# First expert stage of a vision tower on Trainium2: looked-up units copied on chip, first two pairs interleaved

## The reference

```python
h = tok(x)                                     # shifted patches, layernorm, projection
h = h + attn(layernorm(h))                     # 12 heads, fake-quantised
h = h + ffn1(layernorm(h))                     # 8 experts, hidden 512, one expert per token
h = h + block(layernorm(h))                    # state-space block and its own MLP
h = h + ffn2(layernorm(h))                     # 8 experts, hidden 768, two experts per token
```

```python
route = softmax(hidden @ router_w + router_b); e = argmax(route)
out[token] = (silu(x @ w1[e]) * (x @ w2[e])) @ w3[e] * max(route)
```

## Time and profile before

| | us |
|---|---|
| runs | 360.35, 359.46, 364.96 |
| median of the three | 360.35 |
| the profiled execution, its own time | 361.43 |
| its span, first to last instruction | 359.7 |
| TensorE busy | 328.1 |
| VectorE busy | 184.2 |
| ScalarE busy | 136.9 |
| GpSimd busy | 90.5 |

### The profile page before, as it was taken

How to read it: one execution, slowest core, us unless ns; L and a number is a source line. 1 busy time by engine, 2 the same in 40 slices (tenths; PEclk the granted TensorE clock), 3 DMA queues, 4 the chain that set the end, 5 groups by cost and what they waited for, 6 DMA issues and landing times.

```text
span 359.7 us, 6821 instructions
## 1 busy us (share of the span) xinstructions
PE 328.1 (91%) x2564; PEld 252.3 (70%) x2564; DVE 184.2 (51%) x513; ACT 136.9 (38%) x282; POOL 90.5 (25%) x120
## 2 busy tenths in 40 slices
PE   4999998949987999999897988988999999999996
PEld 2999874527553445455674756757999999999995
DVE  3785797775561343467989533574123321521125
ACT  3999222871421122237981433331121121221220
POOL 8299814000014322102032020004223233222110
PEclk9999999977997899999999999999999999999999
DMA  7944349967959999170059993022299999999322
GB/s 235 397 87 104 70 138 273 267 153 220 235 144 254 270 289 243 33 178 20 0 118 294 250 238 90 18 58 58 58 287 284 266 266 274 251 255 248 99 74 86
DMA packets 32450, 64.56 MB, mean 179 GB/s; under 512 B 11009, under 2 KB 17698, under 8 KB 32418
## 3 DMA queue, kind: packets, MB, share of 16 engines
q1 hardware_dynamic: 30210, 59.38, 62.7%
q0 software_dynamic: 1920, 4.56, 4.8%
q10 hardware_dynamic: 288, 0.20, 0.2%
HBM read 59.46 MB, written 4.65 MB: 178 GB/s over the span
## 4 chain that ended last, share of the span: by engine, by line
PE 69%; DVE 12%; ACT 7%; POOL 6%; issue 3%; DMA 1%; another core or an unknown queue 0%; SPq 0%; DVEq 0%; ACTq 0%
PE ps L1850 12%; PE ps L1875 9%; PE ps L1862 7%; PE ps L1941 4%; PE ps L1658 4%; PE ps L1593 4%; PE ps L1974 3%; PE ps L1738 3%; PE ps L1664 2%; PE ps L1949 2%; PE ps L1827 2%; POOL tot L105 1%; PE ps L2152 1%; PE ps L1963 1%; POOL xsq L592 1%
## 5 line engine op out<-in xcount | busy, mean ns | idle before, releaser
L665 POOL DMA_INDIRECT xg<-token_x,src_id x22 | 21.4, 974 | 125.5 <-DVE src_id L1328 79.5
L1357 DVE TENSOR_TENSOR ht<-sg,ps 128x384 f32<-128x384 f32 (+1 forms) x48 | 23.8, 509 | 50.2 <-ACT sg L877 45.6
L1850 PE MATMUL ps<-xgt,wup 128*128 128x128 f32 x384 | 45.6, 275 | 1.5 <-ACT xgt L868 1.5
L1850 PEld LDWEIGHTS ps<-xgt,wup 128*128 128x128 f32 x384 | 44.8, 192 | 2.0 <-issue 2.0
L1593 PE MATMUL ps<-busy 128*128 128x512 bf16 x149 | 41.1, 390 | 4.5 <-POOL ident L575 4.5
L877 ACT ACTIVATE sg<-ps 128x384 f32<-128x384 f32 (+1 forms) x48 | 21.1, 455 | 50.3 <-PE ps L1862 32.7
L1601 PE MATMUL ps<-weff,xp 128*128 128x193 f32 x240 | 39.9, 327 | 0.1
L1601 PEld LDWEIGHTS ps<-weff,xp 128*128 128x128 f32 x240 | 39.2, 190 | 0.7 <-DVE weff L1012 0.7
L1875 PE MATMUL ps<-wdn,ht 128*128 128x192 f32 x192 | 35.2, 334 | 0.0
L672 POOL DMA_INDIRECT token_y<-ysb,row_id x20 | 19.7, 987 | 54.8 <-ACT ysb L884 54.5
L1875 PEld LDWEIGHTS ps<-wdn,ht 128*128 128x128 f32 x192 | 30.8, 190 | 1.8
(11 more groups left out here) (348 smaller groups left out, 563.8 us busy)
## 6 DMA issues: line engine op xcount, KB each, us to landing
wup<-in_m_w SPq DMA_DIRECT2D x16, 576.0 KB
wup<-in_m_w SPq DMA_DIRECT2D x48, 192.0 KB
wdn<-in_m_w SPq DMA_DIRECT2D x16, 576.0 KB
wup<-in_m_w SPq DMA_DIRECT2D x13, 384.0 KB, 6.2
wup<-in_m_w SPq DMA_DIRECT2D x39, 128.0 KB, 6.8
wdn<-in_m_w SPq DMA_DIRECT2D x13, 384.0 KB, 8.6
xw<-in_xw SPq DMA_DIRECT2D x2, 784.0 KB, 10.4
wall<-in_w_sh SPq DMA_DIRECT2D x2, 768.0 KB, 7.3
```

The costliest lines, as they stand in the source:

```text
L665: g.indirect_dma_start(xg[:, j, :], None, token_x[m], bass.IndirectOffsetOnAxis(ap=src_id[:, j:j + 1], axis=0))\
L1357: v.tensor_tensor(ht[:, j % 2, s, 0:half], sg[:, s, 0:half], ups, ALU.mult)\
L1850: mm(ps[:, 2 * s + g, c * P:c * P + P], up[:, col:col + P], xgt[:, 0, j * P:j * P + P], start=(c == 0), stop=False)
```

## The change

Three things change in the first expert stage.

1. Units 8 to 11 no longer come from memory. Once the weights of all own units have arrived, SP copies them from the buffer of the own unit with the looked-up expert to buffers 8 to 11, with two DMAs a unit from SBUF to SBUF. To address that buffer by a register, the nine buffers of the arena become one tensor `w1`; the layout in memory stays.
2. Before SP loads unit 12 (from memory, as before), it waits until units 8 to 11 have arrived, since buffers 0 to 3 may be a copy's source. Semaphore values follow: two DMAs in place of five.
3. Pairs 0 and 1 are interleaved like all others. TensorE does pair 0's up products, three fill matmuls, the transposes of the first gathered group, two fill matmuls, and then pair 1's up products, and pair 0's across and down work inside that iteration. The wait for the remainder rows (`a_f1`) moves to `up_pair_rest(0)`. ACT and DVE follow the same order.

```diff
-W_LOADS = 5
+W_LOADS, C_LOADS = 5, 2
+WARM_ROWS = (3, 2)
...
+        w1 = sb("w1", [P, M1_LOW, UP + DOWN], scope=arena)
...
             b, uses = weight_uses(m, j)
-            return S[ARRIVED[b]], 16 * W_LOADS * uses + (16 if b >= 10 else 0)
+            if m == 0 and b >= E:
+                return S[ARRIVED[b]], 16 * C_LOADS + (16 if b >= 10 else 0)
+            return S[ARRIVED[b]], 16 * W_LOADS * uses
...
+            def copied_weights(j, e):
+
+                b, _ = weight_uses(0, j)
+                up, down = wbuf[0][b]
+                own = w1[:, bass.ds(e, 1), :].rearrange("p e n -> p (e n)")
+                sp.dma_start(up, own[:, 0:UP]).then_inc(S[ARRIVED[b]], 16)
+                sp.dma_start(down, own[:, UP:UP + DOWN].rearrange("p (c d) -> p c d", d=D)).then_inc(S[ARRIVED[b]], 16)
...
                     if j < E:
                         expert_weights(m, j)
+                        continue
+                    if m == 0 and j == E:
+                        for i in range(E):
+                            sp.wait_ge(*weights_here(0, i))
+                    if m == 0 and j == M1_BUFS:
+                        for i in range(E, M1_BUFS):
+                            sp.wait_ge(*weights_here(0, i))
+                    e = sp.value_load(te[0:1, j - E:j - E + 1], min_val=0, max_val=E - 1)
+                    if m == 0 and j < M1_BUFS:
+                        copied_weights(j, e)
                     else:
-                        expert_weights(m, j, sp.value_load(te[0:1, j - E:j - E + 1], min_val=0, max_val=E - 1))
+                        expert_weights(m, j, e)
```

ScalarE, VectorE and TensorE:

```diff
-                    if (m, j) == (0, 0):
-                        result(0)
-                    elif j >= (2 if m == 0 else 1):
+                    if j >= 1:
                         result(j - 1)
...
-                    if m == 0 and j >= 2:
+                    if m == 0 and j >= 1:
                         hidden_across(j - 1)
                     if j == 0:
                         product(0, 0)
-                        if m == 0:
-                            product(0, 1)
-                            hidden_across(0)
                         gathered(1)
-                        if m == 1:
-                            product(0, 1)
+                        product(0, 1)
...
                     pe.wait_ge(S["a_gt"], r["group_of"][j] + 1)
-                    if j == 0:
-                        pe.wait_ge(S["a_f1"], 2)
-                    else:
+                    if j > 0:
                         pe.wait_ge(S["v_gt"], r["group_of"][j])
...
                 def up_pair_rest(j):
 
+                    if j == 0:
+                        pe.wait_ge(S["a_f1"], 2)
...
                         if j == 0:
                             up_pair_rest(0)
-                            hidden_across(0)
-                            down_pair(0)
+                            keep_busy(2, WARM_ROWS[0])
                             gathered(1)
+                            keep_busy(2, WARM_ROWS[1])
                             continue
-                        if j >= 2:
-                            hidden_across(j - 1)
+                        hidden_across(j - 1)
...
                         up_pair_rest(j)
-                        if j >= 2:
-                            down_pair(j - 1)
+                        down_pair(j - 1)
```

More of the change, by code:

```diff
@@ L219, in build @@
         gate = sb("gate", [P, 2, TT])
[L222 to L230, removed]
+        arena = ExitStack()
+        w1 = sb("w1", [P, M1_LOW, UP + DOWN], scope=arena)
+        arena.close()
+        arena = ExitStack()
+        wbuf = [[(w1[:, b, 0:UP], w1[:, b, UP:UP + DOWN].rearrange("p (c d) -> p c d", d=D)) for b in range(M1_LOW)],
+                [(sb(f"wup{b}", [P, 3 * M2_H], scope=arena), sb(f"wdn{b}", [P, M2_H // P, D], scope=arena))
+                 for b in range(M2_BUFS)]]
+        arena.close()
         arena = ExitStack()
```

## The result

The changed kernel's median is 358.75 us in 20 runs (357.74 to 362.66), that of the kernel before 362.04 us in 20 (358.63 to 367.55). The ratio is 0.9938, 95% interval [0.9913, 0.9963]: 0.6% faster, clear of noise; the medians differ by 0.9%, 3.3 us. The forecast was no change (+0.2 us), and its base, the median of three runs, lay 1.7 us under that of the twenty.

What follows compares the result with a forecast made beforehand. TensorE's work was taken to bound the kernel, so only pair 2's start counts: +0.2 us on the profiled 361.43 gives 361.6; that execution being 1.1 us above the three-run median, the forecast median was 360.6, range 357.0 to 364.5.

Steps and rivals of the forecast that it cites:

- 1.6 us to spare: At the new barrier: unit 15's weights come at 144.5, ahead of pair 7's shifted start, so no stall.
- four copies would be down at 123.1: Units 8 to 11: copies priced at this kernel's own stream, 5.1 us a unit; ends 116.6 and 125.2.
- The upper end, 397 GB/s: Copies of units 8 to 11 at the page's fastest slice would be down at 116.6.
- I take 8.1: Pair 1: the gather issued at 109.23 takes 8.1 us, lands at 117.3, and TensorE waits if the clock stays full.
- Rival 2: Copies hold up the gathers: third gather 10.3 us, pair 2 +1.6 to +4.8 us, 362 to 365.2 us; chance 0.13.
- 5.5 forecast: First gather, issued at 106.47: lands at 112.0, the middle between 109.7 and 114.2, the weight stream being three units old.
- I lean to the low clock: Around pair 1: clock low as before, pair 2 starts at 122.0, 1.0 us later; with possible earlier return, +0.2 us.
- SP's eight waits: Ahead of the copies: waits for the units' own weights cost only their issue, 0.3 us; first copy at 102.65.
- rival 3: Copies at half rate, 130 GB/s, land at 141; unit 15 at 162.4, +16.3 us, 376.7 us; chance 0.08.

Runs made afterwards that it cites:

- e9: The kernel before, unchanged, profiled a second time: one run, 363.96 us.
- e1: The changed kernel without its copies (units 8 to 11 loaded from memory by five DMAs again; new order and fill matmuls stay): ratio to the kernel before 0.9995.
- e4: The kernel before with fill matmuls in pair 0's two stalls, order and loads as before: ratio to the kernel before 0.9991.
- e6: The changed kernel with unit 12 loaded twice from memory, so that the stream of weights ends later: ratio to the kernel before 1.0163.
- e8: The changed kernel with units 10 and 11 copied only when the second and third gather have landed: ratio to the kernel before 0.9981.
- e14: The changed kernel, unchanged, measured and profiled again: ratio to the kernel before 0.9945, median 360.93 us.
- e5: The kernel before with the weights of units 12 to 15 left out but for 32 columns of each piece: ratio to the kernel before 1.0001.
- e10: The kernel before with first-stage weights packed in memory as in a buffer, two DMAs a unit, old order, no copies: ratio to the kernel before 0.9885.
- e7: The changed kernel with each unit copied in the five pieces of a load from memory instead of two: ratio to the kernel before 1.0140.
- e3: The changed kernel without the fill matmuls around the first gathered transposes: ratio to the kernel before 0.9955.
- e2: The changed kernel with the old order on TensorE, ACT and DVE and no fills; copies and barrier stay: ratio to the kernel before 0.9928.
- e15: The changed kernel with the old order, copies and barrier kept, run a second time: ratio to the kernel before 0.9995.
- e11: The changed kernel's order with fills, weights packed in memory, no copies on chip: ratio to the kernel before 0.9981.
- e12: The changed kernel with its copies and barrier, and packed weights for the units still loaded from memory: ratio to the kernel before 0.9887.

## Why the prediction was wrong, point by point

1. **The step that failed: "Pair 7 starts at 145.92 [...]: 1.6 us to spare, where there were 2.9."** From this followed that only the start of pair 2 counts, and pair 2 was forecast 0.2 us later. I read the slack of the weight stream from one execution and took it for the kernel's. In e9 unit 15 was complete at 148.03 and TensorE stood for 3.50 us; e1 and e4, with the same loads, waited too. The slack was also read too wide: I took the end of the stream from the DMA share (143.0), and where a landing is on record it comes 1.3 to 2.3 us later than that (e9: 145.7 by the share, 148.03 landed; e6: 146.3 and 148.43; e8: 144.3 and 145.6). So pair 7's weights were the limit in three of the four profiles with the loads of the kernel before, and ending the stream sooner was worth something. e6 shows the converse: a longer stream alone puts the changed kernel 0.9 to 1.6% above the kernel before.

   But this is one of two ways to the gain. Between e9 and e14 (on different chips) it is all of it: pair 2 at 12.74 and 12.83, pair 7 at 41.21 and 37.57. Between the two first profiles it is none: pair 2 gained 2.8 us (14.49 to 11.73) and pair 7 the same 2.8, with no wait in either. That is the failure of points 3 and 4, the third gather and the clock, from which the sum had its +0.2. Either way pair 7 starts 2.8 to 3.6 us sooner, and the medians fell by 3.3 and 3.0. How often an execution goes which way no run shows, and e5's ratio doesn't confirm the first.
2. **"5.1 us a unit [...] four copies would be down at 123.1."** They ran mostly at 403 to 407 GB/s and were down at 118.7. The upper end, 397 GB/s, was the right row. The rule that I cited ("DMA: Bandwidth & Descriptors" in the Trainium skill, section Bandwidth: HBM at about 358, inside SBUF 435) gave 115.5, nearer than my value, but for a reason that the runs don't bear out: e10 drew 384 to 420 GB/s from memory, and e7's copies inside SBUF made 247 to 299. The same section gives the 358 for two cores that stream at once, and one core ran here; I had left that condition out. What decided was how the transfer is cut.
3. **"The nearest price is that of the two gathers behind it [...]; I take 8.1."** Right for loads from memory in five pieces (8.31, 8.38), wrong beside the copies (5.98). Rival 2, longer rows hold up the gathers, didn't come: the first gather landed 5.1 us after its issue, against 5.5 forecast. (The 5.5 came out near, but its reason was misread: SP had issued one unit and begun the second by then, not three.)
4. **"I lean to the low clock."** It stayed full in the changed kernel's profile, fell for a part of pair 1 in e14 and e3, not at all in e2, and for all of pair 1 in e15; in the kernel before it fell in the first profile and not in e9. That goes with 1.1 us (12.83 against 11.73) to 2.9 us (e15 against e2) of pair 2's start. The same kernel did both, so it isn't a property of the order or the fills alone.
5. **Right:** `up_pair(0)` is no longer held by the remainder rows; TensorE idles 2 us ahead of the first gathered transposes, and the third gather then leads the chain; SP's eight waits cost nothing that shows; rival 3, copies at half rate, didn't come; no change of 2%.

Open: how much the new order adds to the copies. Together 0.9938 and 0.9945, copies alone 0.9928 and 0.9995; the second pair scatters by more than the difference. Open too: why the stream of one and the same program moved 270 GB/s in one execution and 255 in another, and whether the chip or chance did it.

## What to carry to other kernels

Slack that one profile shows on a transfer is a sample, and a busy share that falls is not yet a landing: profile the kernel a second time before an argument rests on 3 us of it, above all where runs scatter by 2% and the other engines repeat to a tenth of a microsecond. Where a stream of loads is near the limit, first look at how it is cut, and at what its semaphore counts: a wait for a whole unit waits for pieces that the next step doesn't read (e9). In the copies two DMAs of 128 partitions moved 1.3 to 1.6 times (403/299 to 407/247) what five DMAs, four of them on parts of the partitions, did; loads from memory gained in the same way, and this needs only another layout in memory. The copies had one thing that the packed loads had not, quicker gathers beside them. An order that shortens the start of a stage pays only if its last loads arrive sooner as well (e4, e8).

## What the runs showed of the hardware

- DMA into SBUF by the cut: five pieces over 96, 32, 64, 64 and 128 partitions 230 to 299 GB/s, from memory or from SBUF; two pieces over 128 partitions mostly 346 to 424 from memory (down to 264 in single stretches with gathers and scatters among them) and 383 to 416 from SBUF (means over 3 us with the queues full). Row length and partition span changed together, so which of them does it is open.
- Gathers of 128 rows, issue to landing, third of the stage: 8.2 us beside five-piece loads from memory (e5), 6.4 beside packed loads from memory (e11), 5.5 to 5.9 beside copies from SBUF in five or two pieces (e7; e6, e12), 2.8 with the copies held back (e8).
- A wait of 2.5 to 4.6 us ahead of pair 7 is paid twice: behind it the clock fell to the lower level for a time in e4, e6, e7, e8 and e9, and pair 7's first half took 2.65 to 3.57 us. In e1, after 1.83 us, it took 1.94.
- At one place the same program fell to the low clock or not, with idle pieces alike to 0.15 us: the kernel before for 6.8 us and not at all (e9), the copies alone for not at all (e2) and 6.8 us (e15), the changed kernel not at all and for 3.4 us (e14).
